# GQA: the projection sum gets another PSUM bank, scores are computed query-major, matmuls of the multi-query attention alternate, last tiles use spare banks

## What is computed

```python
# layer 0, attention (GQA): 16 query heads, 4 key/value heads of 128
q = _layernorm(q, qn_g, qn_b); k = _layernorm(k, kn_g, kn_b)
q = q * cos + _rotate_half(q) * sin
k = k * cos + _rotate_half(k) * sin
scores = jnp.einsum('bhqd,bhkd->bhqk', q, k) / jnp.sqrt(jnp.float32(D))
scores = jnp.where(causal, -jnp.inf, scores)
weights = jax.nn.softmax(scores, axis=-1)
attn = jnp.einsum('bhqk,bhkd->bhqd', weights, v)
return jnp.einsum('bsd,od->bso', attn.transpose(0, 2, 1, 3).reshape(b, s, H * D), w_o)
# layer 1, attention (multi-query): 16 query heads, one key/value head, of 16
scores = jnp.einsum('bqhd,bkd->bhqk', q, k) * scale       # causal softmax
ctx = jnp.einsum('bhqk,bkd->bqhd', attn, v); out = ctx @ out_w.T + out_b
# layer 1, cross attention: 16 heads of 128 on the context, then o_w
```

## Time and profile before

| | |
|---|---|
| median of 3 runs | 3430.74 us (3427.8 to 3444.24) |
| profiled execution | 3426.8 us, its span 3424.9 us |
| busy in the span | PE 2791.3 us (81%), DVE 2082.8 (61%), POOL 1604.7 (47%), ACT 1579.4 (46%) |
| GQA, 78 to 1008 us | PE 755 busy of 930, POOL 697, DVE 660, ACT 517, granted clock 0.99 |
| multi-query attention, 1632 to 2018 us | PE 351 busy of 386, granted clock 0.84 |
| cross attention, 2040 to 3134 us | PE 1028 busy of 1094, granted clock 0.98 |

### The profile page before, as it was taken

The page is one execution under the profiler, slowest core; times in us unless marked ns, Lnnn a source line. Parts: engine busy times, 40 slices in busy tenths (PEclk is TensorE's granted clock), DMA queues, the critical chain, the costliest instruction groups (busy, mean ns, idle before and its releaser), DMA issues. The chain is left out here.

```text
span 3424.9 us, 84976 instructions
## 1 busy us (share of the span) xinstructions
PE 2791.3 (81%) x32044; PEld 2022.4 (59%) x32044; DVE 2082.8 (61%) x3786; ACT 1579.4 (46%) x2718; POOL 1604.7 (47%) x1643
## 2 busy tenths in 40 slices
PE   1788888888858888866899978999999999995565
PEld 1666666666642222223777767888888788784232
DVE  4677777777748888847566653444444444443776
ACT  2555555555526777731333333333333333331665
POOL 1777777777742323223222214545455454551332
PEclk9899999999987999979788879999999999997666
DMA  3000000000002332200000000000000000000000
GB/s 112 1 0 0 0 0 0 0 0 0 0 25 81 92 96 87 86 12 10 22 21 21 21 21 4 7 5 7 5 7 7 6 7 5 7 2 26 13 18 18
DMA packets 94065, 73.24 MB, mean 21 GB/s; under 512 B 17314, under 2 KB 88354, under 8 KB 93218
## 3 DMA queue, kind: packets, MB, share of 16 engines
q1 hardware_dynamic: 93860, 70.14, 6.8%
HBM read 51.76 MB, written 17.04 MB: 20 GB/s over the span
## 5 line engine op out<-in xcount | busy, mean ns | idle before, releaser
L1296 DVE TENSOR_REDUCE x_mx<-x_ps 128x2 f16<-128x512 f32 x512 | 331.3, 682 | 50.2 <-PE x_ps L1360 47.5
L1265 ACT ACTIVATE x_e<-x_ps 128x512 f32<-128x512 f32 x512 | 292.0, 596 | 50.4 <-PE x_ps L1364 34.4
L1639 ACT ACTIVATE x_sq<-x_ps 128x512 f32<-128x512 f32 x256 | 152.1, 595 | 309.8 <-PE x_ps L1778 303.0
L1360 PE MATMUL x_ps<-x_k,x_q 32*128 32x256 f16 x1024 | 196.3, 286 | 80.8 <-ACT x_e L1265 49.3
L540 POOL TENSOR_TENSOR a_w<-a_qsw,a_tab 128x512 f32<-128x512 f32 x128 | 218.5, 1707 | 7.3 <-ACT a_qsw L600 6.3
L1360 PEld LDWEIGHTS x_ps<-x_k,x_q 32*128 32x128 f16 x1024 | 58.2, 93 | 263.7 <-DVE x_mx L1296 132.4
L103 PE MATMUL x_ps<-x_chi,x_w 128*128 128x128 f16 x1024 | 200.2, 221 | 14.4 <-ACT x_rkb L1660 7.5
L103 PE MATMUL x_ps<-ln_xhx,x_w 128*128 128x128 f16 x1024 | 198.2, 219 | 1.7 <-DVE x_k L1698 1.7
L104 PE MATMUL x_ps<-x_clo,x_w 128*128 128x128 f16 x1024 | 199.5, 220 | 0.0
L105 PE MATMUL x_ps<-x_chi,x_w 128*128 128x128 f16 x1024 | 199.3, 220 | 0.0
L1364 PE MATMUL x_ps<-x_q,x_k 32*128 32x256 f16 x1024 | 197.7, 287 | 1.7 <-ACT x_e L1265 1.4
(11 more groups left out here) (346 smaller groups left out, 9680.4 us busy)
## 6 DMA issues: line engine op xcount, KB each, us to landing
x_q<-x_q_rows SPq DMA_DIRECT2D x32, 256.0 KB, 2.8
x_k<-x_k_rows SPq DMA_DIRECT2D x32, 256.0 KB, 3.1
a_stage<-in_x_w SPq DMA_DIRECT2D x32, 256.0 KB, 2.6
x_vt<-in_ctx_v SPq DMA_DIRECT2D x32, 144.0 KB, 2.3
x_all<-in_x SPq DMA_DIRECT2D x8, 512.0 KB, 7.4
x_cf<-in_ctx SPq DMA_DIRECT2D x32, 128.0 KB, 2.1
x_q_rows<-x_xhl SPq DMA_DIRECT2D x32, 128.0 KB, 1.8
x_k_rows<-x_chl SPq DMA_DIRECT2D x32, 128.0 KB, 1.8
```

The costliest lines, as they stand in the source:

```text
L1265: act.activation(e[:, u % ES].rearrange("p c n -> p (c n)"), s2_ps(u), ACT.Exp, scale=XT ** -0.5).then_inc(e_ready, 1)
L1296: dve.reduce_max(mx[:, p % 2, c:c + 2], s1_ps(u), AX).then_inc(mx_ready, 1)
L1360: return pe.matmul(s1_ps(u)[:, c], q[r, p % 4, g, c * P:(c + 1) * P], k[r, p % 4, g], start=True, stop=True)
L1639: act.activation(sq[:, e % 4, :], ps[:, bank(e), :], ACT.Square).then_inc(act_left, 1)
```

## The change

In GQA, `y` moves from bank 4 to bank 0, and queries' group 2 from bank 0 to bank 4. The turning of probabilities no longer waits for `x_done`, and the first projection waits for `kt_ready` of the next tile, because `keys_scaled` reads bank 0; group 2 of the queries waits for the scores to have left bank 4. Scores are computed with queries on the partitions at once, by 32 matmuls of 64 columns in place of 8 of 256; the copy to `st` and `turn_scores` go. On PE the sums of squares come before the layer norm's transposes and the scores, and the first values before group 0 of the queries; group 2 comes before the first projection, whose second half of values follows it. On ScalarE `at_.high` 0 comes before `square` 0. In the multi-query attention the two halves alternate from matmul to matmul. In GQA and cross attention the last tiles take spare banks, so that both halves of values run before the first projection. The lines of the new file are up to 16 higher.

```diff
-    def __init__(self, m, ctx, sem, tag, ps, w_out, v_cols):
+    def __init__(self, m, ctx, sem, tag, ps, w_out, v_cols, y_bank=4):
...
-        self.o = self.ob.rearrange("p b h s -> p h b s")
-        self.y = ps[:, 4, 0:DM]
+        self.y = ps[:, y_bank, 0:DM]
+
+        self.spare_ptp = ps[:, 0:2, :].rearrange("p k (h s) -> p (k h) s", s=P) if y_bank else self.ptp
+        self.spare_ob = ps[:, 2:4, :].rearrange("p b (h s) -> p b h s", s=SEQ)
+
+    def by_seq(self, r, spare):
+
+        return self.spare_ob if spare and r else self.ob
...
-    def transpose(self, pe, t, left):
+    def transpose(self, pe, t, left, spare=False):
         pe.wait_ge(self.p_ready, t + 1)
-        wait_used(pe, left, t, 1)
+        if not spare:
+            wait_used(pe, left, t, 1)
         ev = self.e[:, :, :].rearrange("p (k b) s -> p k (b s)", b=2)
...
+        elif spare:
+            pe.wait_ge(self.v_ready, self.v_count * TILES)
+            pe.wait_ge(self.ol_ready, 2 * t)
         else:
             pe.wait_ge(self.ol_ready, 2 * t + 1)
+        ob = self.by_seq(r, spare)
...
-    def project(self, pe, t, r, last_tile=False):
+        o = self.by_seq(r, spare).rearrange("p b h s -> p h b s")
+        dve.tensor_tensor(split(self.ol), o, split(self.oh), ALU.subtract).then_inc(self.ol_ready, 1)
+
+    def project(self, pe, t, r, last_tile=False, bank_free=None):
         pe.wait_ge(self.ol_ready, 2 * t + 1 + r)
-        if r == 0 and not last_tile:
+        if r == 0 and last_tile:
+            pe.wait_ge(self.x_done, t)
+        elif r == 0 and bank_free is not None:
+            pe.wait_ge(bank_free, t + 3)
+        elif r == 0:
...
-        at_ = Attend(m, ctx, sem, "a0", ps, wo, NK)
+        at_ = Attend(m, ctx, sem, "a0", ps, wo, NK, 0)
...
-        QBANK = (2, 1, 0, 3)
+        QBANK = (2, 1, 4, 3)
...
-            def scores_out(t):
-                act.wait_ge(stp_ready, t + 1)
-                wait_used(act, at_.sc_ready, t, 1)
-                act.copy(st[:, :, :], sct).then_inc(st_ready, 1)
...
-                scores_out(t)
                 if has_next:
                     square_keys(t + 1)
-                    square(t + 1, 0)
                 if before:
                     at_.high(act, t - 1, 0)
                 if has_next:
+                    square(t + 1, 0)
+                if has_next:
                     square(t + 1, 1)
                 at_.exponential(act, t)
...
-                    pe.wait_ge(kt_ready, t + 1)
+                    wait_used(pe, at_.sc_left, t, 1)
...
-                for g in range(KV):
+                for k in range(PAIRS):
                     for b in range(2):
-                        keys_ = slice(g * HD + b * SEQ, g * HD + (b + 1) * SEQ)
-                        last = pe.matmul(sct[b * SEQ:(b + 1) * SEQ, 4 * g:4 * g + 4, :], kt[:, keys_],
-                                         u[:, b, 4 * g:4 * g + 4, :], start=True, stop=True)
-                last.then_inc(stp_ready, 1)
-
-            def turn_scores(t):
-                pe.wait_ge(st_ready, t + 1)
-                for k in range(PAIRS):
-                    last = pe.transpose(at_.ptp[:, k, :], st[:, 2 * k:2 * k + 2, :].rearrange("p h s -> p (h s)"), m.ident[:, :])
+                        first_key = (k // 2) * HD + b * SEQ
+                        for h in range(2):
+                            last = pe.matmul(at_.sc[h * SEQ:(h + 1) * SEQ, 2 * k + b, :], u[:, b, 2 * k + h, :],
+                                             kt[:, first_key:first_key + SEQ], start=True, stop=True)
                 last.then_inc(at_.sc_ready, 1)
...
-                    at_.transpose(pe, t - 1, at_.x_done)
-                if has_next:
                     pe.wait_ge(u_ready, 4 * t + 3)
+                    at_.transpose(pe, t - 1, None, True)
+                bias_scores(t)
+                query_sums(t)
+                if has_next:
+                    if before:
+                        wait_used(pe, at_.x_done, t - 1, 1)
                     ln.transpose(pe, t + 1, 1 - p)
-                bias_scores(t)
                 scores(t)
-                query_sums(t)
                 if has_next:
                     keys(t + 1, 1 - p)
                     value(t + 1, 1 - p)
                     key_sums(t + 1)
-                    queries(t + 1, 1 - p, 0)
-                turn_scores(t)
                 if before:
                     pe.wait_ge(vq_ready, t + 1)
                     at_.values(pe, t - 1, 1 - p, 0)
                 if has_next:
+                    queries(t + 1, 1 - p, 0)
                     queries(t + 1, 1 - p, 1)
                     key_factors(t + 1)
-                if before:
-                    at_.project(pe, t - 1, 0)
+                    queries(t + 1, 1 - p, 2)
+                if before and has_next:
+                    at_.project(pe, t - 1, 0, False, kt_ready)
                     at_.values(pe, t - 1, 1 - p, 1)
-                if has_next:
-                    queries(t + 1, 1 - p, 2)
+                elif before:
+                    at_.values(pe, t - 1, 1 - p, 1, True)
+                    at_.project(pe, t - 1, 0, True)
+                if has_next:
                     queries(t + 1, 1 - p, 3)
                 if before:
                     at_.project(pe, t - 1, 1)
             over_tiles(pe, head, step)
             t, p = TILES - 1, 1
-            at_.transpose(pe, t, at_.x_done)
-            for r in range(2):
-                at_.values(pe, t, p, r)
-                at_.project(pe, t, r, True)
+            at_.transpose(pe, t, None, True)
+            at_.values(pe, t, p, 0)
+            at_.values(pe, t, p, 1, True)
+            at_.project(pe, t, 0, True)
+            at_.project(pe, t, 1, True)
...
+                halves = [slice(c * SEQ, (c + 1) * SEQ) for c in range(2)]
                 for a in range(2):
-                    for c in range(2):
-                        rows = slice(c * SEQ, (c + 1) * SEQ)
-                        for b in range(2):
-                            tok = slice(b * SEQ, (b + 1) * SEQ)
-                            out = sc[rows, a * 8 + b:a * 8 + 8:2, :]
-                            pe.matmul(out, m.identb[:, rows], repeat(maskb[:, :], 4), start=True, stop=False)
-                            last = pe.matmul(out, qk[:, p, c, tok], kd[:, 4 * a:4 * a + 4, tok], start=False, stop=True)
+                    for b in range(2):
+                        tok = slice(b * SEQ, (b + 1) * SEQ)
+                        out = sc[:, a * 8 + b:a * 8 + 8:2, :]
+                        for rows in halves:
+                            pe.matmul(out[rows], m.identb[:, rows], repeat(maskb[:, :], 4), start=True, stop=False)
+                        for c, rows in enumerate(halves):
+                            last = pe.matmul(out[rows], qk[:, p, c, tok], kd[:, 4 * a:4 * a + 4, tok], start=False, stop=True)
-                for b in range(2):
-                    rows = slice(b * SEQ, (b + 1) * SEQ)
-                    for k in range(AG):
+                for k in range(AG):
+                    for b in range(2):
+                        rows = slice(b * SEQ, (b + 1) * SEQ)
                         last = pe.matmul(o_ps[:, b, k * AD:(k + 1) * AD], pt[rows, k, :], v[rows, p, :], start=True, stop=True)
                 last.then_inc(pv_ready, 1)
```

More of the change, by code:

```diff
@@ L407, in values @@
                 for b, rows in halves:
-                    last = pe.matmul(self.ob[:, b, 4 * j:4 * j + 4, :], self.v[rows, p, g * HD:(g + 1) * HD],
+                    last = pe.matmul(ob[:, b, 4 * j:4 * j + 4, :], self.v[rows, p, g * HD:(g + 1) * HD],
                                      self.pt[rows, 2 * g:2 * g + 2, :].rearrange("p k (h s) -> p (k h) s", s=SEQ),
@@ L486, in attention_gqa @@
         sql = sb("sql", [P, 2, HEADS, SEQ], BF16)
-        st = sb("st", [P, HEADS, SEQ])
         sqk = sb("sqk", [P, NK])
@@ L632, in step @@
                 if before:
-                    at_.high(act, t - 1, 1)
+                    at_.high(act, t - 1, 1, not has_next)
                 if has_next:
@@ L637, in _ @@
             over_tiles(act, head, step)
-            at_.copy_transposed(act, TILES - 1)
+            at_.copy_transposed(act, TILES - 1, True)
             at_.high(act, TILES - 1, 0)
-            at_.high(act, TILES - 1, 1)
+            at_.high(act, TILES - 1, 1, True)
         @block.vector
@@ L730, in step @@
                 if before:
-                    at_.low(dve, t - 1, 1)
+                    at_.low(dve, t - 1, 1, not has_next)
                 if further(t):
@@ L747, in _ @@
             at_.low(dve, TILES - 1, 0)
-            at_.low(dve, TILES - 1, 1)
+            at_.low(dve, TILES - 1, 1, True)
             at_.add(dve, TILES - 1)
@@ L1860, in step @@
                     front(t + 1, 1 - p, range(2, 4))
-                if before:
+                if before and has_next:
                     at_.project(pe, t - 1, 0)
                     at_.values(pe, t - 1, 1 - p, 1)
```

(12 more changed lines are left out.)

32 lines of the change are left out of this document (16 added, 16 removed).

## The result

The changed kernel takes 3516.34 us (median of 4 runs, 3502.12 to 3534.04), the kernel before 3432.97 in the same comparison: ratio 1.0241, interval 1.0183 to 1.0298: slower; whether by more than 2% the interval leaves open. The medians lie 83.4 us apart. The profiled execution, the fastest of the four, took 3502.12 us, its span is 3500.3 against 3424.9, so +75.4 us; what follows explains these 75.4.

The account below looks back on a forecast made before the run. GQA's round was taken to close through GpSimd, with 1.0 us to spare before the first projection. Terms 75 + 30 - 23 - 15 = +67 us on 3426.8 gave 3494 us, whole range 3400 to 3568.

Parts of the forecast that it names:

- The wait for the bank: GQA: the first projection, waiting for `kt_ready`, lengthens each round by 2.5 us; 75 us over 30 rounds (42 to 102).
- GpSimd's waits for the statistics and for ScalarE's swapped copy: GQA, signs expected in the changed profile: GpSimd waits for the layer norm's statistics and for ScalarE's swapped copy.
- +17.1: GQA: `kt_ready` comes 17.1 us after the end of GpSimd's fourth `squares_low`; the projection starts 3.9 us later than before.
- slack: GQA: the first projection's start has 1.0 us to spare; what delays it more lengthens the round.
- The clock in GQA: GQA: two PE idle gaps a round can drop the clock, up to 1.7 us each; taken as 1.0 a round, 30 us.
- falls in both gaps of each round: Rival, GQA: the clock falls before the first projection and before the sums every round; +141 us, 3568; chance 0.07.
- Query-major scores: GQA: 64 instructions of 64 columns take 2.13 us against 1.95, as in cross attention; keys start no later; taken as 0.
- Multi-query attention: Its 31 rounds: scores' second half starts 0.35 us earlier, products give 0.4 to 0.6; together 0.75 a round, -23 us.
- the clock's up to 62 us: Multi-query attention: if the clock, at 0.84, stopped falling, 62 us more would come back; not counted on.
- Last tiles: GQA and cross attention, two tiles each: 2.37 us waits before the second projection go, values fill earlier waits; -15 us (0 to -20).

Follow-up runs that it names:

- the filled kernel: Changed kernel with unused matmuls in both GQA idle gaps of PE, before the first projection and before the sums of squares: 3449.71 us, ratio 1.0043.
- the kernel with before's rounds: Kernel before with GQA's rounds kept, plus alternating halves in multi-query attention and spare banks for last tiles in GQA and cross attention: 3363.96 us, ratio 0.9791.
- earlier release: Changed kernel, but the first projection waits only for the keys' first multiplication, the one that reads bank 0: 3442.38 us, ratio 1.0019.
- first filling alone: Changed kernel with 16 unused matmuls between queries' group 2 and the first projection, nothing before the sums of squares: 3448.04 us, ratio 1.0034.
- the kernel with both repairs: Changed kernel with the projection waiting only for the keys' first multiplication, and unused matmuls before the projection and before the sums: 3442.04 us, ratio 1.0039.

## Why the prediction held, and which terms were wrong

Slower, and the size nearly as forecast (+75.4 against +67 on the profiled execution, +83.4 by medians), but the sum owes its closeness to luck: two large errors, 55 us too little for GQA's clock and 27 us too little for the gain in multi-query attention, offset each other, and 12 us came off where it had no term.

- *The wait for the bank, 2.5 a round, 75 us.* Right in place and size. `kt_ready` releases the projection, as forecast 3 to 4 us a tile, and so do GpSimd's waits for the statistics and for ScalarE's swapped copy. With the clock at 1.00 it costs 2.12 a round (66 us in 31), with the old scores and order 2.28 in the rounds in which the clock holds. But its derivation fell. `kt_ready` was to come at +17.1, later than before, because the values stand ahead of group 0; undoing that order brings nothing, and with the scores at full speed it comes at +16.7, where it was before. (What releases it, the keys' last multiplication in the prediction's words, is the addition of the bias behind it.) The projection is late because it waits for it at all, and its slack was 1.4 us, not 1.0. In the changed profile `kt_ready` is at +18.3, since the slow scores push the keys back: VectorE waits 5.16 us for their swapped copy, and the scores' product queues behind that.
- *The clock in GQA, 1.0 a round, 30 us.* **This is the mis-sized term.** It costs 2.74 a round, 85 us. The text priced one slow burst at up to 1.7 and took 1.0 for both gaps; the projection is 1.65 us longer and all of it counts (1.7 a round), and the slow scores cost 1.0 more. So the case "falls in both gaps of each round", which had little chance, comes near to GQA: before the projection in 30 of 30 tiles, before the scores in 25 of 31. The Trainium skill (TensorE: Matmul & The Clock Gate, HAM oscillation) said this of bursts with idle gaps between them; here the trace agrees for the gap of 3.73 us, while behind gaps of 2.39 and 3.02 us the clock fell in 3 and 6 of 30 tiles.
- *Query-major scores, 0.* 2.08 us at full clock against 2.13 from cross attention: the row was right. The Trainium skill (TensorEngine Tiling (Array Packing), Instruction Overhead) gave an estimate of 3.3 us, by adding the page's 60 cycles to the 64 columns; the changed profile does show 3.33, but mostly at 1.2 GHz, and the filled kernel's 2.08 decides against that sum. The section also says that a matmul of 1 column takes as long as one of 60; read as a floor, this gives an estimate of 64 x 64 cycles, 1.7 us, to which the 2.08 lies nearer. What the 0 missed: alone they cost 0.26 a round, and they widen the gap before the projection from 3.0 to 3.7 us, with which the clock falls in every tile instead of every fifth.
- *Multi-query attention, -23 us.* Measured -50. The shorter instructions were counted nearly right (9 + 22 us separately), and the clock's up to 62 us were named but not counted on, on the ground that the matmuls and the idle time together stay as long. They don't: together they went from 386 to 336 us, PE's busy time from 351 to 263, and only with both alternations does the clock stop falling.
- *Last tiles, -15 us.* In the changed profile -5.2 in GQA and -12.4 in the last two tiles of cross attention, whose stage gains 8.1 in all; in the kernel with before's rounds -6.8 and -14.8. What goes beyond the 15 there was again the clock, 0.50 in projections that the sum took at full speed.
- *Sum of the changed profile:* 150.4 in GQA's rounds (66 at full clock, 85 clock) - 7.5 - 5.2 - 3.9 - 49.6 - 8.1 - 0.7 = 75.4, as between the spans. The 7.5 by which GQA's first scores' product comes earlier, and the 3.9 and 0.7 in stages with the same code, were in no term.

## What to carry to other kernels

When a change shortens PE's work in front of a wait, price the gap that it leaves as well as the work: here 0.7 us more idle time in front of one matmul group made it slow in 30 tiles of 30 instead of six, at 1.7 us each. A wait for a bank is to be hung on the instruction that reads the bank, not on the last of the helper that contains it. Parts of a change are to be measured alone: here one part hid the 50 and 18 us that two others gave.

## What had not been expected of the hardware

- Whether the clock falls behind a gap depends on more than its length. Behind the same gap of 2.56 us before the sums, the scores were slow in 25, 31 and 13 of 31 tiles (the change, earlier release, first filling alone), and behind the same 3.02 us the projection was slow in 6 of 30. A single tile's row tells neither that the clock falls nor that it holds.
- Unused matmuls in GQA raised its clock and shortened it by 85 us, but part was missing at the end: later stages with the same instructions took longer. That is not shown to come from the filling. The features and LoRA stages took 623.9 us in the changed kernel at a clock of 0.91, 627 to 629 in nine others, and 641.1 at 0.87 with the earlier release, which has no filling and lost a part of its gain there too (53 us between the profiled spans, 74 between the medians). In cross attention, in the kernel with both repairs, PE's idle time without a visible cause before the same transposes doubled (51.9 against 23.3 us), though the filling stands in GQA alone. Its cause stays open. The Trainium skill (Runtime: NRT & Kernel Launch, Instruction fetch mechanics) says that a taken branch to code outside the fetched pages stalls an engine; no run here shows whether that is it.
